# Edge-network pass: the inner layer with its features on the partitions, subtraction and dots on TensorE, floor on ScalarE

## The chip, the core and the metric

The kernel runs on one NeuronCore of a Trainium2 chip. The core has five engines that run side by side: TensorE (matrix products, written to PSUM), VectorE, ScalarE, GpSimd and SyncE; they signal each other by semaphores. The metric is the device time of one execution in microseconds, start to end. TensorE's clock has two levels here, 1.2 and 2.4 GHz; the profile gives the granted clock as a share of the higher one, so that 0.50 is 1.2 GHz.

## What is computed

Four graph layers over 6250 nodes of 128 features and 106,250 edges, sorted by target. The third is the one that matters here:

```python
def _L2_gnn_ref(x, src, dst, W1, b1, W2, b2, W4, b4):
    theta = x[dst] - x[src]
    w = sigmoid(relu(theta @ W1 + b1) @ W2 + b2)        # W2 is 128 x 1
    agg = segment_sum(w * theta, dst)
    indeg = segment_sum(ones, dst)
    return agg + indeg * (x @ W4 + b4)
```

Since theta @ W1 + b1 is (x @ W1 + b1)[dst] - (x @ W1)[src], the layer before it leaves two tables in DRAM: `rows_yh`, with y = x @ W1 and h = x side by side for each node, and `parts_yb`, with x @ W1 + b1 cut into three bf16 parts (high, middle, low) whose sum is the fp32 value.

## The kernel before

`edge_pass` with `edge_net` set is the pass in question. The edges are cut into 832 tiles of 128; 4 tiles are a group (GROUP), 16 a turn (RING, one ring of buffers), so there are 52 turns and 208 groups. In what follows n is a group's number. All targets of a group lie in a window of 64 nodes. The program is unrolled; its order on each engine is that of the code: `over` calls each engine's work for a tile (`tile`, on TensorE `net_tile`) and puts a share of the block's work (`Layer2.on_pe`, `on_dve` and so on, the last product and normalisation of 128 finished nodes) between tiles, at about one block in 4 groups (a step).

What is done for a group, by engine:

- GpSimd (L557): for each tile a gather of 128 rows of `rows_yh` into `ring[:, k]`, edges on the partitions. It may overwrite slot k when by_target of the group that used it is done (`tiles_done`), so it runs up to four groups ahead.
- ScalarE: loads the window's rows of `parts_yb` into `ywin` (L578) and the targets into `relb` (L570); copies by_target out of PSUM (`held_sums`, L585); takes the sigmoid of the dots into `weight` (L597).
- VectorE: `one_hots` makes for 8 tiles `onehot_t` (64 targets on the partitions by edges, L631) and `onehot` (edges by targets, L633). `dots` takes zt - y of the source (L640), the floor at zero times W2, which is spread over all partitions (L643), and the sum over the 128 features (L648). `onehot_w` is onehot times weight (L658). `add_sums` adds the group's sums to `acc` (L687, L689).
- TensorE: `hidden_net` of the next group (L719) spreads the three parts of `ywin` to the edges: per tile three bf16 products into zt[edge, feature] (64 rows contracted, 128 columns); then `turn_sums` of the group before (L729, L730), and `by_target` of this group (L750), four fp32 products that sum weight times h over the edges.

An fp32 product appears in the trace as two weight loads and two products (passes), a bf16 product as one of each.

So within one group's time TensorE runs z of n+1, the turns of n-1 and by_target of n. VectorE runs onehot_w of n, the dots of n+1 and the add of n-1; by_target of n waits for onehot_w of n (semaphore `weighted`), that for the sigmoid (`weight_done`), that for the dots (`dot_done`), those for z (`z_done`). `zt` has two halves, for even and odd groups.

Before the pass, `Layer1.late_dve` makes the y that goes into `rows_yh` (`next_y`), and `expert_tables` loads W2 once.

Of the kernel before, what the change touches and what calls it, by code (L numbers as in the profile page):

```python
# [7 lines left out]
D = 128  # L8
# [4 lines left out]
P = 128  # L13
# [137 lines left out]
def gnn_kernel(nc, t, out):  # L151
    ctx = ExitStack()
    with ctx:
# [284 lines left out]
        def edge_pass(table, width, work, edge_net=None, prologue=None):  # L438
# [11 lines left out]
            with ExitStack() as tmp:  # L450
# [9 lines left out]
                if edge_net:  # L460
                    (w2, b2) = edge_net
                    onehot_t = tmp.enter_context(sbuf("onehot_t", [WIN, 2, HALF * P], B16))
                    relb = tmp.enter_context(sbuf("relb", [WIN, 2, HALF * P]))
                    ywin = tmp.enter_context(sbuf("ywin", [WIN, GROUPS, PARTS * D], B16))
                    hidden = tmp.enter_context(sbuf("hidden", [P, GROUP, D]))
                    dot = tmp.enter_context(sbuf("dot", [P, 2, GROUP]))
# [5 lines left out]
                    names += ["rel_loaded0", "rel_loaded1", "z_done", "net_own", "dot_done", "weight_done",  # L472
                              "weighted", "copied", "turned"] + [f"ywin_loaded{g}" for g in range(GROUPS)]

                def programs(block, sems, loop):
# [87 lines left out]
                    def _(act):  # L563
# [23 lines left out]
                        def tile(i, k):  # L587
                            g, q = divmod(k, GROUP)
                            if edge_net and q == 0:
# [15 lines left out]
                        over(act, tile, flush=(lambda: copy_sums(LAST_GROUP)) if edge_net else None)  # L605
# [14 lines left out]
                    def _(dve):  # L620
# [14 lines left out]
                        def dots(i, g):  # L635

                            n = i * (2 * GROUPS) + 2 * g
                            k = g * GROUP
                            dve.wait_ge(sem["z_done"], i * GROUPS + (g + 1))
                            nc.vector.tensor_tensor(hidden[:, :, :], zt[:, g % 2, :, :], ring[:, k:k + GROUP, 0:D],  # L640
                                                    ALU.subtract).then_inc(sem["net_own"], 1)
                            dve.wait_ge(sem["net_own"], n + 1)
# [4 lines left out]
                            dve.wait_ge(sem["net_own"], n + 2)  # L647
# [3 lines left out]
                        def tile(i, k, ahead=True):  # L651
# [14 lines left out]
                            if edge_net and (ahead or g < GROUPS - 1):  # L666

                                dots(i + (g + 1) // GROUPS, (g + 1) % GROUPS)
# [26 lines left out]
                        if edge_net:  # L695
                            if loop == "edges":
                                nc.vector.memset(ring[:, :, YH:YH + 1], 1.0)
                                dots(0, 0)
                            over(dve, tile, lambda i, k: tile(i, k, ahead=False), lambda: add_sums(LAST_GROUP))
# [4 lines left out]
                    def _(pe):  # L704
# [4 lines left out]
                        def hidden_net(i, k):  # L709
# [23 lines left out]
                        def net_tile(i, k, ahead=True):  # L733

                            g, q = divmod(k, GROUP)
                            if k + GROUP < RING:
                                hidden_net(i, k + GROUP)
# [37 lines left out]
                        if loop == "edges":  # L775
                            pe.sem_inc(tiles_done, RING)
                            if edge_net:
                                for k in range(GROUP):
                                    hidden_net(0, k)
# [226 lines left out]
        class Layer1(Work):  # L1006
# [315 lines left out]
            def late_dve(self, dve, m, i, b):  # L1322
# [30 lines left out]
                m.done("next_y", nc.vector.tensor_copy(s["yh"][:, 0:D], p["misc"][:, 0:D]))  # L1353
# [1270 lines left out]
        w4, b4, w2, b2 = (net.enter_context(sbuf(n, s)) for n, s in (("w4", [P, D]), ("b4", [P, D]), ("w2", [P, D]),  # L2624
                                                                     ("b2", [P, 1])))
        with ExitStack() as lay:
            def weight(name, shape):
# [7 lines left out]
                                    (w2[:, :], bcast_vec(t["L2_gnn_W2"].rearrange("p o -> (p o)"))),  # L2635
# [44 lines left out]
```

## Time and profile before

| | us |
|---|---|
| median of 3 runs | 7054.21 |
| lowest and highest | 7053.46, 7054.47 |
| span of the profiled execution | 8283.1 |

The page knows no other time of the profiled execution than its span from the first to the last instruction. It is 1228.9 us longer than the median of the runs without a profile, so a duration taken from the trace is that of the longer execution. The page gives for every engine busy time, for 40 slices of the span the granted clock of TensorE, and the costliest groups of instructions with the idle time just before them and what ended it. PE is TensorE, PEld its weight loads, DVE VectorE, ACT ScalarE, POOL GpSimd; SPq, ACTq and POOLq are their DMA queues. Idle time that ends with a semaphore is put down to the instruction that released it; semaphores are used again in later phases, so a name such as "DMA acc<-in_edge_type", a load of the setup phase, can stand here for a release that the profile couldn't place.

### The profile page before, as it was taken

How to read it: one execution, taken by the hardware profiler on the slowest of the kernel's cores; microseconds unless marked ns; L12 is line 12 of the kernel's file. 1: busy time of each engine (PE TensorE's matmuls, PEld its weight loads, DVE VectorE, ACT ScalarE, POOL GpSimd, SP SyncE). 2: the span in 40 equal slices, each digit the busy share in tenths (PEclk: the TensorE clock that was granted, in tenths of full speed). 3: DMA queues.
4: the chain of work that ended last, by engine and by line, in shares of the span. 5: the costliest groups of instructions: out<-in, count | busy, mean ns of one | idle time of the engine just before them, and what ended most of it. 6: DMA issues, size and time to landing. Idle time of an engine off the chain costs nothing. (4 is left out here: it accounts for less than half of the span.)

```text
span 8283.1 us, 149959 instructions
## 1 busy us (share of the span) xinstructions
PE 6772.3 (82%) x51098; PEld 4970.7 (60%) x51098; DVE 3911.7 (47%) x11484; ACT 2104.7 (25%) x6166; POOL 3351.8 (40%) x3404
## 2 busy tenths in 40 slices
PE   4999768888886888888688888867767766989899
PEld 2555457676775677677567776755555554545455
DVE  7777534444443444444344554446666662112111
ACT  3555312222221222222133333322222220000000
POOL 0000055555554555555455555536666661000000
PEclk6999879999997999999799999975555557999999
DMA  5444355554444544445444444434444445656565
GB/s 152 139 119 126 115 160 145 143 143 140 140 129 148 143 142 140 138 143 147 133 135 138 141 138 136 139 89 124 128 124 124 126 124 187 196 170 198 175 202 161
DMA packets 714971, 1188.63 MB, mean 144 GB/s; under 512 B 258882, under 2 KB 512998, under 8 KB 712163
## 3 DMA queue, kind: packets, MB, share of 16 engines
q0 software_dynamic: 200640, 601.97, 26.1%
q1 hardware_dynamic: 466786, 447.42, 18.0%
q10 hardware_dynamic: 46784, 129.65, 4.4%
q8 instruction: 411, 6.73, 0.3%
q14 instruction: 350, 2.86, 0.1%
HBM read 993.57 MB, written 185.20 MB: 142 GB/s over the span
## 5 line engine op out<-in xcount | busy, mean ns | idle before, releaser
L557 POOL DMA_INDIRECT ring<-parts,src_idx x2496 | 2452.0, 982 | 1950.7 <-PE sums L707 687.1
L1209 PEld LDWEIGHTS hid<-agg,big 128*128 128x128 f32 x9408 | 1155.6, 196 | 140.2 <-issue 105.9
L1209 PE MATMUL hid<-agg,big 128*128 128x128 f32 x9408 | 1190.6, 280 | 58.8 <-issue 43.5
L2360 PE MATMUL agg_ps<-sheet,big 128*128 128x448 f16 x6174 | 1196.4, 354 | 33.6 <-DMA sheet<-adj 33.6
L1170 PE MATMUL y<-big,strong 128*128 128x256 f32 x4704 | 1126.2, 387 | 40.6 <-issue 21.3
L557 POOL DMA_INDIRECT ring<-rows_yh,src_idx x832 | 838.0, 1007 | 565.4 <-issue 220.3
L677 DVE TENSOR_TENSOR acc<-acc,sums 128x128 f32 x624 | 180.3, 289 | 1678.6 <-DMA acc<-in_edge_type 1171.4
L2360 PEld LDWEIGHTS agg_ps<-sheet,big 128*128 128x128 bf16 x6174 | 605.9, 99 | 582.5 <-DMA sheet<-adj 35.8
L1170 PEld LDWEIGHTS y<-big,strong 128*128 128x128 f32 x4704 | 862.7, 191 | 150.9 <-issue 51.4
L1093 ACT ACTIVATE strong<-hid,s_b 128x128 f32<-128x128 f32 x2352 | 665.3, 368 | 892.6 <-PE hid L1209 615.2
L707 PE MATMUL sums<-onehot,ring 128*128 128x64 bf16 x14976 | 614.5, 196 | 284.1 <-issue 211.6
L707 PEld LDWEIGHTS sums<-onehot,ring 128*128 128x128 bf16 x14976 | 563.2, 100 | 433.6 <-issue 390.5
L1195 PE MATMUL hid<-big,agg 128*128 128x512 f32 x1176 | 747.8, 768 | 64.7 <-DVE agg L1108 53.5
L750 PE MATMUL by_target<-ring,onehot_w 128*64 128x129 f32 x1664 | 408.7, 427 | 131.3 <-DVE onehot_w L658 103.5
L750 PEld LDWEIGHTS by_target<-ring,onehot_w 128*64 128x64 f32 x1664 | 328.5, 223 | 176.9 <-issue 176.3
L1098 DVE SCALAR_TENSOR_TENSOR row<-y,gate,row 128x256 f32<-128x256 f32 x588 | 282.8, 481 | 319.0 <-DMA adj<-big 230.0
L1945 PE MATMUL counts_ps<-hot_col,hot 128*128 128x392 bf16 (+3 forms) x1960 | 348.3, 299 | 102.1 <-DVE hot_col L1804 97.9
L1195 PEld LDWEIGHTS hid<-big,agg 128*128 128x128 f32 x1176 | 254.0, 239 | 272.6 <-issue 212.1
L1073 ACT ACTIVATE weak<-weak 128x512 f32<-128x512 f32 x294 | 185.0, 629 | 866.9 <-DVE weak L1117 778.5
L1776 POOL MEMSET acc<- 128x10976 f32 x1 | 9.2, 9244 | 933.8 <-PE deg_ps L1945 933.8
L2472 DVE SCALAR_TENSOR_TENSOR agg<-agg_ps,counts_hold,acc 128x448 f32<-128x448 f32 x42 | 28.7, 684 | 724.7 <-PE agg_ps L2360 724.7
L2416 POOL MEMSET acc<- 128x448 f32 (+1 forms) x28 | 13.4, 479 | 874.1 <-DVE agg L2472 874.1
(377 smaller groups left out, 8497.9 us busy)
## 6 DMA issues: line engine op xcount, KB each, us to landing
sheet<-adj SPq DMA_DIRECT2D x294, 784.0 KB, 4.2
ring<-parts,src_idx POOLq DMA_INDIRECT x2496
adj<-big ACTq DMA_DIRECT2D x7, 5488.0 KB
adj<-acc ACTq DMA_DIRECT2D x7, 5488.0 KB
hp<-parts SPq DMA_DIRECT2D x147, 192.0 KB
relb<-rel_rows ACTq DMA_DIRECT2D x106, 256.0 KB
parts<-cut SPq DMA_DIRECT2D x99, 192.0 KB, 1.8
h<-rows SPq DMA_DIRECT2D x147, 128.0 KB
```

The source lines that it names most:

```text
L557: nc.gpsimd.indirect_dma_start(ring[:, k, 0:YH] if edge_net else ring[:, k, :], None, table, bass.IndirectOffsetOnAxis(ap=src_idx[:, i * R ...
L677: nc.vector.tensor_tensor(acc[:, 0:n_sums, bass.ds(w, WIN)], acc[:, 0:n_sums, bass.ds(w, WIN)], sums[:, g % 2, 0:n_sums * WIN].rearrange(" ...
L707: return nc.tensor.matmul(ap, lhs, rhs, start=first, stop=last, skip_group_check=True)
L750: last = nc.tensor.matmul(by_target[:, g % 2, 0:D + 1], onehot_w[:, g % 2, j, :], ring[:, g * GROUP + j, D:YH + 1], start=(j == 0), stop=( ...
L1073: m.done(f"relu_w{q}", nc.scalar.activation(both, both, ACT.Relu))
L1093: ins = nc.scalar.activation(s["strong"][:, e % 2, j, :], p["hid"][:, bank_at, j * P:(j + 1) * P], ACT.Relu, bias=self.w["s1_b"][:, e, j:j ...
L1098: m.done(name, nc.vector.scalar_tensor_tensor(out=out, in0=expert, scalar=self.b[0]["gate"][:, e:e + 1], in1=so_far, op0=ALU.mult, op1=ALU ...
L1170: ins = nc.tensor.matmul(y, s["strong"][:, e % 2, k, :], w["s2"][:, k, e, :], start=(k == 0), stop=(k == 3))
L1195: ins = nc.tensor.matmul(hid, s["agg"][:, k, :], w["weak"][:, k, 2 * q:2 * q + 2, :].rearrange("p e f -> p (e f)"), start=(k == 0), stop=( ...
L1209: ins = nc.tensor.matmul(p["hid"][:, bank_at, j * P:(j + 1) * P], w["s1"][:, k, e, j * P:(j + 1) * P], s["agg"][:, k, :], start=(k == 0), ...
L1945: return nc.tensor.matmul(ap, lhs, rhs, start=first, stop=last, skip_group_check=True)
L2360: last = nc.tensor.matmul(ps[:, g % 2, 0:HALF_COLS], now[:, b, c, :], sheet[:, k, s * HALF_COLS:(s + 1) * HALF_COLS], start=(b == 0 and c ...
```

## The change

The inner layer of the network is turned round: features on the partitions, edges along the row.

- `hidden_net`: for a group, three products of `ywin` (as weights) with `onehot_t` over 512 edges give zt[feature, edge]; then for each tile a fp32 product of the gathered y (as weights) with the identity adds to it. `next_y` now stores -y, so this subtracts. z of group n+1 waits in addition for `weight_done` of n-1, since the dots of n-1 stand in the same half of zt. Only the tile products wait for the gathers.
- ScalarE gets `relu_hidden`: the floor of zt, 128 by 512, into `hidden` (two halves now), behind `z_done`.
- TensorE gets `dots`: four fp32 products, `hidden` of a tile as weights with W2 as a single column, into the first four columns of zt; they follow the first tile product of the next group.
- VectorE loses its three steps. The sigmoid reads the dots from PSUM. W2 is loaded as a column of 128 by 1.

```diff
@@ ScalarE @@
-                        def tile(i, k):
+                        def tile(i, k, ahead=True):
...
-                                nc.scalar.activation(weight[:, g % 2, :], dot[:, g % 2, :], ACT.Sigmoid,
+                                nc.scalar.activation(weight[:, g % 2, :], zt[:, g % 2, 0, 0:GROUP], ACT.Sigmoid,
                                                      bias=b2).then_inc(sem["weight_done"], 1)
+                            if edge_net and q == GROUP - 1 and (ahead or g < GROUPS - 1):
+                                relu_hidden(i * GROUPS + g + 1)
+
+                        def relu_hidden(n):
+                            act.wait_ge(sem["z_done"], n + 1)
+                            nc.scalar.activation(hidden[:, n % 2, :], zt[:, n % 2, :, :].rearrange("p q j -> p (q j)"),
+                                                 ACT.Relu).then_inc(sem["hidden_done"], 1)
@@ VectorE @@
-                        def dots(i, g):
...
-                            nc.vector.tensor_tensor(hidden[:, :, :], zt[:, g % 2, :, :], ring[:, k:k + GROUP, 0:D],
-                                                    ALU.subtract).then_inc(sem["net_own"], 1)
...
-                            nc.vector.scalar_tensor_tensor(
-                                out=hidden[:, :, :], in0=hidden[:, :, :], scalar=0.0,
-                                in1=w2.unsqueeze(1).to_broadcast([P, GROUP, D]), op0=ALU.max,
-                                op1=ALU.mult).then_inc(sem["net_own"], 1)
...
-                            nc.vector.tensor_reduce(dot[:, g % 2, :], hidden[:, :, :], AX.X,
-                                                    ALU.add).then_inc(sem["dot_done"], 1)
@@ TensorE, hidden_net @@
-                            pe.wait_ge(gathered[k], i * 16 + 16)
                             if q == 0:
                                 pe.wait_ge(sem[f"ywin_loaded{g}"], i * 16 + 16)
-                            for c in range(PARTS):
-                                last = nc.tensor.matmul(zt[:, g % 2, q, :], onehot_t[:, g // 2, (k % HALF) * P:(k % HALF + 1) * P],
-                                                        ywin[:, g, c * D:(c + 1) * D], start=(c == 0), stop=(c == PARTS - 1))
+                                if not first:
+                                    pe.wait_ge(sem["weight_done"], i * GROUPS + g - 1)
+                                for c in range(PARTS):
+                                    nc.tensor.matmul(zt[:, g % 2, :, :].rearrange("p q j -> p (q j)"), ywin[:, g, c * D:(c + 1) * D],
+                                                     onehot_t[:, g // 2, (k % HALF) * P:(k % HALF + GROUP) * P],
+                                                     start=(c == 0), stop=False, skip_group_check=True)
+                            pe.wait_ge(gathered[k], i * 16 + 16)
+                            last = nc.tensor.matmul(zt[:, g % 2, q, :], ring[:, k, 0:D], ident[:, :], start=False, stop=True,
+                                                    skip_group_check=True)
...
+                        def dots(n):
+                            pe.wait_ge(sem["hidden_done"], n + 1)
+                            for q in range(GROUP):
+                                last = nc.tensor.matmul(zt[:, n % 2, 0, q:q + 1], hidden[:, n % 2, q * P:(q + 1) * P],
+                                                        w2, start=True, stop=True)
+                            last.then_inc(sem["dot_done"], 1)
@@ TensorE, net_tile @@
+                            if q == 0:
+                                dots(n)
...
-                m.done("next_y", nc.vector.tensor_copy(s["yh"][:, 0:D], p["misc"][:, 0:D]))
+                m.done("next_y", nc.vector.tensor_scalar(s["yh"][:, 0:D], p["misc"][:, 0:D], -1.0, None, ALU.mult))
...
-                                    (w2[:, :], bcast_vec(t["L2_gnn_W2"].rearrange("p o -> (p o)"))),
+                                    (w2[:, :], t["L2_gnn_W2"]),
```

The order on the engines. Output<-inputs are the program's names, then the shape of the output; of the semaphores that a row waits for, signal18 is `z_done`, signal19 `net_own` before and `hidden_done` in the change, signal20 `dot_done`, signal21 `weight_done`, signal22 `weighted`, signal23 `copied`, signal2 `added`, signal26 `ywin_loaded1`, signal1 `tiles_done`.

TensorE, one group in the middle of the pass, before:

```order
L719 MATMUL zt<-ywin,onehot_t 128x128 [waits signal26,gathered4]
L719 MATMUL zt<-ywin,onehot_t 128x128 x2
L719 MATMUL zt<-ywin,onehot_t 128x128 [waits gathered5]
L719 MATMUL zt<-ywin,onehot_t 128x128 x2
L719 MATMUL zt<-ywin,onehot_t 128x128 [waits gathered6]
L719 MATMUL zt<-ywin,onehot_t 128x128 x2
L729 MATMUL sums<-ident,held_sums 128x64 [waits signal2,signal23]
L730 MATMUL sums<-ident,held_sums 1x64
L719 MATMUL zt<-ywin,onehot_t 128x128 [waits gathered7]
L719 MATMUL zt<-ywin,onehot_t 128x128 x2
L750 MATMUL by_target<-ring,onehot_w 64x129 [waits signal22,signal23]
L750 MATMUL by_target<-ring,onehot_w 64x129 x3
```

and in the change:

```order
L710 MATMUL zt<-onehot_t,ywin 128x512 [waits signal21,signal26]
L710 MATMUL zt<-onehot_t,ywin 128x512 x2
L714 MATMUL zt<-ident,ring 128x128 [waits gathered4]
L723 MATMUL zt<-w_72,hidden 128x1 [waits signal19]
L723 MATMUL zt<-w_72,hidden 128x1 x3
L714 MATMUL zt<-ident,ring 128x128 [waits gathered5]
L714 MATMUL zt<-ident,ring 128x128 [waits gathered6]
L732 MATMUL sums<-ident,held_sums 128x64 [waits signal2,signal23]
L733 MATMUL sums<-ident,held_sums 1x64
L714 MATMUL zt<-ident,ring 128x128 [waits gathered7]
L755 MATMUL by_target<-ring,onehot_w 64x129 [waits signal22,signal23]
L755 MATMUL by_target<-ring,onehot_w 64x129 x3
```

Twelve products of 128 columns are now three of 512, four more follow with one gather to wait for each, and the four dots stand behind the first of these, with the turns and two tile products between them and by_target.

ScalarE, the group in which a block's square root is taken, before:

```order
L585 COPY held_sums<-by_target 64x129 [waits signal24,signal1]
L597 ACTIVATE weight<-dot,b_73 128x4 [waits signal20]
L898 ACT_TABLE_LOAD
L898 ACTIVATE st<-st 128x1 [waits signal9]
L901 ACTIVATE h_178<-x,st 128x128 [waits signal9]
L503 TENSOR_LOAD step_block
L503 ISA x2
```

and in the change:

```order
L597 ACTIVATE weight<-zt,b_73 128x4 [waits signal20]
L903 ACT_TABLE_LOAD
L903 ACTIVATE st<-st 128x1 [waits signal9]
L906 ACTIVATE h_178<-x,st 128x128 [waits signal9]
L605 ACTIVATE hidden<-zt 128x512 [waits signal18]
L503 TENSOR_LOAD step_block
L503 ISA x2
```

The floor is the last step of each group's turn; in this group of four it stands behind the block's L903 and L906 (L898 and L901 before), and the next group's loads stand behind it.

VectorE, one group, before:

```order
L658 TENSOR_TENSOR onehot_w<-onehot,weight 128x256 [waits signal1,signal21]
L640 TENSOR_TENSOR hidden<-zt,ring 128x512 [waits signal18]
L643 SCALAR_TENSOR_TENSOR hidden<-hidden,w_72 128x512 [waits signal19]
L648 TENSOR_REDUCE dot<-hidden 128x4 [waits signal19]
L684 TENSOR_LOAD win
L684 ISA x2
L687 ISA [waits signal2,signal24]
L687 TENSOR_TENSOR acc<-acc,sums 1x64
L689 ISA
L689 TENSOR_TENSOR acc<-acc,sums 128x64
```

and in the change:

```order
L652 TENSOR_TENSOR onehot_w<-onehot,weight 128x256 [waits signal1,signal21]
L675 TENSOR_LOAD win [waits signal3]
L675 ISA x2
L678 ISA [waits signal2,signal24]
L678 TENSOR_TENSOR acc<-acc,sums 1x64
L680 ISA
L680 TENSOR_TENSOR acc<-acc,sums 128x64
```

The three network steps are gone; onehot_w is followed at once by the add.

## Rows read from the trace of the kernel before

**Rows 1.** The page, part 2: granted TensorE clock in 40 slices, tenths.

```profile
PEclk6999879999997999999799999975555557999999
```

**Rows 2.** One line's own view, for L557 and L719: times, then total us and times of waits.

```profile
  DMA acc<-in_edge_type: 651.3, 337
...
L719 PE MATMUL zt<-ywin,onehot_t x2496: 259/311/311, 5540.9 to 6865.7; 64*128 64x128 bf16 x192
```

**Rows 3.** Busy time by window: PE, PEld, DVE, ACT, POOL, then clock, DMA share, GB/s.

```profile
5700.00:6700.00 1000.00, 707.61 (x3836) 512.62 (x3837) 656.22 (x1656) 241.23 (x610) 634.54 (x630) 0.50 0.45 125
...
5703.34:5714.10 10.76, 10.76 (x58) 7.83 (x58) 4.91 (x12) 1.90 (x8) 7.39 (x8) 0.50 0.44 125
```

**Rows 4.** Groups by line, 5700 to 6700: busy us, mean ns | idle before, by whom.

```profile
L557 POOL DMA_INDIRECT ring<-rows_yh,src_idx x630 | 635.7, 1009 | 365.8 <-issue 167.1 <-DMA acc<-in_edge_type 121.5 <-PE by_target L750 77.2
...
L750 PE MATMUL by_target<-ring,onehot_w 128*64 128x129 f32 x1259 | 309.4, 427 | 102.8 <-DVE onehot_w L658 79.0 <-issue 23.5
...
L643 DVE SCALAR_TENSOR_TENSOR hidden<-hidden,w 128x512 f32<-128x512 f32 x157 | 108.9, 694 | 5.4
...
L648 DVE TENSOR_REDUCE dot<-hidden 128x4 f32<-128x512 f32 x157 | 107.7, 686 | 5.4
...
L640 DVE TENSOR_TENSOR hidden<-zt,ring 128x512 f32<-128x512 f32 x157 | 107.5, 685 | 229.4 <-remote 221.2 <-issue 6.8 <-PE zt L719 1.2
...
L658 DVE TENSOR_TENSOR onehot_w<-onehot,weight 128x256 f32<-128x256 f32 x158 | 67.5, 427 | 34.9 <-issue 21.6 <-ACT weight L597 7.0 <-DMA acc<-in_edge_type 4.0
```

**Rows 5.** Timeline, TensorE, 5707 to 5714: start us, us, instruction.

```profile
5707.10 0.48 PE L1428 MATMUL pb<-ident,agg 128*128 128x128 f32 x1
...
5708.43 1.14 PE L719 MATMUL zt<-ywin,onehot_t 64*128 64x128 bf16 x9
...
5709.36 0.31 PE L729 MATMUL sums<-ident,held_sums 64*128 64x64 f32 x1
...
5709.90 0.50 PE L719 MATMUL zt<-ywin,onehot_t 64*128 64x128 bf16 x3
...
5710.33 1.98 PE L750 MATMUL by_target<-ring,onehot_w 128*64 128x129 f32 x8
...
5712.24 0.80 PE L1434 MATMUL pa<-w,ht 128*128 128x128 f32 x2
...
5712.97 1.14 PE L719 MATMUL zt<-ywin,onehot_t 64*128 64x128 bf16 x9
```

**Rows 6.** Timeline, other engines, 5713 to 5717.

```profile
5713.47 0.94 POOL L557 DMA_INDIRECT ring<-rows_yh,src_idx  x1 [0.30 <-issue]
...
5715.41 0.69 DVE L640 TENSOR_TENSOR hidden<-zt,ring 128x512 f32<-128x512 f32 x1 [5.96 <-remote]
...
5716.94 0.94 POOL L557 DMA_INDIRECT ring<-rows_yh,src_idx  x1 [2.53 <-DMA acc<-in_edge_type]
```

**Rows 7.** Timeline, TensorE, in an expert layer, 2208 to 2222.

```profile
2208.07 1.02 PE L1221 MATMUL misc<-router,ht 128*128 128x9 f32 x4 [0.24 <-ACT ht L1067]
...
2208.95 1.00 PE L1221 MATMUL misc<-router,agg 128*128 128x9 f32 x4
...
2220.16 1.95 PE L1209 MATMUL hid<-agg,big 128*128 128x128 f32 x16
...
2221.95 0.22 PE L707 MATMUL sums<-onehot,ring 128*128 128x64 bf16 x2
```

**Rows 8.** L1073's own view, and ScalarE's timeline at 5721.

```profile
L1073 ACT ACTIVATE weak<-weak x294: 612/630/633, 1117.4 to 5508.9; 128x512 f32<-128x512 f32 x147
...
5721.50 0.20 ACT L898 ACTIVATE st<-st 128x1 f32<-128x1 f32 x1 [2.32 <-DVE st L889]
```

**Rows 9.** Busy time by window, columns as in rows 3.

```profile
64.43:67.87 3.44, 3.39 (x11) 1.39 (x12) 3.44 (x2) 0.00 (x0) 0.00 (x0) 0.50 0.00 0
...
67.87:71.28 3.41, 3.41 (x22) 1.68 (x20) 3.31 (x15) 0.00 (x0) 0.00 (x0) 1.00 0.69 288
...
2208.00:2211.40 3.40, 3.33 (x10) 2.54 (x11) 2.88 (x8) 0.02 (x1) 2.12 (x3) 0.51 0.37 103
```

More of the change, by code:

```diff
@@ L461, in edge_pass @@
                     (w2, b2) = edge_net
+                    assert w2.shape[1] == 1
                     onehot_t = tmp.enter_context(sbuf("onehot_t", [WIN, 2, HALF * P], B16))
@@ L464, in edge_pass @@
                     ywin = tmp.enter_context(sbuf("ywin", [WIN, GROUPS, PARTS * D], B16))
-                    hidden = tmp.enter_context(sbuf("hidden", [P, GROUP, D]))
-                    dot = tmp.enter_context(sbuf("dot", [P, 2, GROUP]))
+                    hidden = tmp.enter_context(sbuf("hidden", [P, 2, GROUP * P]))
                     weight = tmp.enter_context(sbuf("weight", [P, 2, GROUP]))
@@ L471, in edge_pass @@
                     held_sums = tmp.enter_context(sbuf("held_sums", [WIN, 2, D + 1]))
-                    names += ["rel_loaded0", "rel_loaded1", "z_done", "net_own", "dot_done", "weight_done",
+                    names += ["rel_loaded0", "rel_loaded1", "z_done", "hidden_done", "dot_done", "weight_done",
                               "weighted", "copied", "turned"] + [f"ywin_loaded{g}" for g in range(GROUPS)]
@@ L604, in _ @@
                                     load_window(0, k)
-                        over(act, tile, flush=(lambda: copy_sums(LAST_GROUP)) if edge_net else None)
+                                relu_hidden(0)
+                        over(act, tile, lambda i, k: tile(i, k, ahead=False),
+                             flush=(lambda: copy_sums(LAST_GROUP)) if edge_net else None)
                         if edge_net and loop == "edges":
@@ L633, in one_hots, with tile @@
                             nc.vector.tensor_tensor(onehot[:, h, :, :], places, cols, ALU.is_equal).then_inc(onehot_ready, 1)
-                        def dots(i, g):
-                            n = i * (2 * GROUPS) + 2 * g
-                            k = g * GROUP
-                            dve.wait_ge(sem["z_done"], i * GROUPS + (g + 1))
-                            nc.vector.tensor_tensor(hidden[:, :, :], zt[:, g % 2, :, :], ring[:, k:k + GROUP, 0:D],
-                                                    ALU.subtract).then_inc(sem["net_own"], 1)
-                            dve.wait_ge(sem["net_own"], n + 1)
-                            nc.vector.scalar_tensor_tensor(
-                                out=hidden[:, :, :], in0=hidden[:, :, :], scalar=0.0,
-                                in1=w2.unsqueeze(1).to_broadcast([P, GROUP, D]), op0=ALU.max,
-                                op1=ALU.mult).then_inc(sem["net_own"], 1)
-                            dve.wait_ge(sem["net_own"], n + 2)
-                            nc.vector.tensor_reduce(dot[:, g % 2, :], hidden[:, :, :], AX.X,
-                                                    ALU.add).then_inc(sem["dot_done"], 1)
-                        def tile(i, k, ahead=True):
+                        def tile(i, k):
                             g, q = divmod(k, GROUP)
@@ L665, in tile @@
                                 return
-                            if edge_net and (ahead or g < GROUPS - 1):
-                                dots(i + (g + 1) // GROUPS, (g + 1) % GROUPS)
                             if edge_net:
@@ L697, in _ @@
                                 nc.vector.memset(ring[:, :, YH:YH + 1], 1.0)
-                                dots(0, 0)
-                            over(dve, tile, lambda i, k: tile(i, k, ahead=False), lambda: add_sums(LAST_GROUP))
+                            over(dve, tile, flush=lambda: add_sums(LAST_GROUP))
                         else:
@@ L707, in tile_sum, with hidden_net @@
                             return nc.tensor.matmul(ap, lhs, rhs, start=first, stop=last, skip_group_check=True)
-                        def hidden_net(i, k):
+                        def hidden_net(i, k, first=False):
                             g, q = divmod(k, GROUP)
@@ L736, in net_tile @@
                             if k + GROUP < RING:
-                                hidden_net(i, k + GROUP)
+                                hidden_net(i, k + GROUP, first=i * GROUPS + g < 1)
                             elif ahead:
@@ L778, in _ @@
                                 for k in range(GROUP):
-                                    hidden_net(0, k)
+                                    hidden_net(0, k, first=True)
                         if edge_net:
@@ L2623, in gnn_kernel @@
         net = ctx.enter_context(ExitStack())
-        w4, b4, w2, b2 = (net.enter_context(sbuf(n, s)) for n, s in (("w4", [P, D]), ("b4", [P, D]), ("w2", [P, D]),
+        w4, b4, w2, b2 = (net.enter_context(sbuf(n, s)) for n, s in (("w4", [P, D]), ("b4", [P, D]), ("w2", [P, 1]),
                                                                      ("b2", [P, 1])))
```

## The prediction

> **What bounds the kernel now.** I read the page first: TensorE's clock row stands at 7 to 9 nearly everywhere, but at 5 in one block of six slices [rows 1]. That block is the edge-network pass: its products over zt start between 5540.9 and 6865.7 [rows 2], so 208 groups of four tiles take some 1325 us. The change touches nothing else that runs often. In the 1000 us from 5700 TensorE was busy 707.61 us at a clock of 0.50 (1.2 GHz), VectorE 656.22, ScalarE 241.23 and GpSimd 634.54 [rows 3]. The by_target products came 1259 times, 8 to a group, so there were 157 groups: 6.37 us each, of which TensorE worked 4.5, VectorE 4.2, GpSimd 4.0.
>
> Who waits for whom is in the groups by line: by_target stood idle for 102.8 us of these 1000, 79.0 of them for onehot_w, and GpSimd for 365.8 us before its gathers [rows 4]. VectorE's three network steps cost 685 + 694 + 686 ns = 2.07 us a group [rows 4], but the products of the next group and the sums of this one run meanwhile. **So no engine is full**; the pass is a ring of handovers in which TensorE is the longest member, and that in its slow clock.
>
> One wait I can't name. In the turn that I show, TensorE's last product for zt starts at 5709.90 and by_target ends by 5712.31 [rows 5], but L640, which needs zt alone, starts at 5715.41 after 5.96 us of idleness, and the gather that needs by_target's slots at 5716.94 [rows 6]. GpSimd has 337 such waits, 651.3 us, in the whole span [rows 2], so it isn't this pass alone. The profiled execution spans 1228.9 us more than the median of 7054.21; these stalls may be what profiling adds. I carry them both ways below.
>
> **The change, part by part** (a group; durations from start to start at clock 0.50).
>
> *TensorE, before.* z: nine products in 0.93 us and three in 0.43, 1.36. The two turns 0.54. by_target 1.91. The block's work, once in a little over four groups, 1.33 + 0.73, so 0.5 [rows 5]. Sum 4.3.
>
> *z turned round.* Twelve products of 128 columns become three of 512: the same 1536 columns. Nine weight loads go, but they lay beside products. 1.3 us, gain 0 to 0.1.
>
> *The subtraction.* It adds four fp32 products, 128 by 128, two passes each. From below: by_target's eight passes of 129 columns took 1.91, 0.24 a pass, so 0.48 a product. The same shape (L1209) at full clock ran 16 passes in 1.79 us, 0.11 each, doubled 0.22, which says the same. From above: L1434, same shape at 0.50 but standing alone, its weight load not hidden, took 0.73 [rows 5, 7]. Four cost 1.9 to 2.9; I take 1.9, since they follow other products whose time hides the load, as in L1209.
>
> *The dots.* Four fp32 products with one column, so only weights are loaded: eight passes. L1221 (nine columns, clock 0.50) started its next four passes 0.88 us after the first four, 0.22 a pass; with the end of the last counted in, 1.02 or 0.26 [rows 7]. 1.8 to 2.1; I take 1.8, the pace of a row of them.
>
> TensorE after: 1.3 + 1.9 + 1.8 + 0.54 + 1.91 + 0.5 = **8.0 us a group** (7.9 to 9.3), 3.7 more.
>
> *VectorE* loses 2.07 us a group. Nobody is served by that: it had 2.1 us to spare.
>
> *ScalarE* gains a floor over 128 by 512; L1073, a ScalarE step of that shape, took 630 ns in the median [rows 8]. It isn't waited for: between z_done(n) and dots(n) stand by_target(n-1), z and one subtraction, 1.91 + 1.3 + 0.5 us. After the dots come three subtractions and the turns, 2.0 us, before by_target asks for weights that need one short ScalarE step and 0.43 us of onehot_w [rows 4]: hidden, but for the table load that the sigmoid has once a step. In one group of four the floor is queued behind the block's square root (L898, L903 in the change), which waits for VectorE's statistics, 2.32 us in the row [rows 8]; those now come sooner, as VectorE is freer. The order has as many table loads as before, so the floor adds none. z's new wait for weight_done(n-1) is met a by_target earlier.
>
> *Gathers.* z no longer waits for them, only the subtraction does; the wait moves inside the same group, nothing gained. The column load of W2 and the sign in next_y cost the same within a microsecond in all.
>
> *Sum.* TensorE goes from 4.5 busy plus 1.9 idle to 8.0 to 8.2 busy plus whatever idleness is left. If all hidden waits go and the unnamed stall too, a group is 8.2 and the profiled pass grows 208 x (8.2 - 6.37) = 381 us; if the stall stays (about 4 us in four groups, 1.0), 9.2 and 589 us. For runs without a profile I scale the pass by 7054/8283: 1325 becomes 1128 us, 5.42 a group. TensorE alone then sets 8.0: 208 x 8.0 = 1664, **+536 us**, 7590. From that I take off 20 us for short stretches at full clock: **7570**.
>
> **The clock** decides. In the pass now TensorE never left 0.50, not even from 5703.34 to 5714.10, when it was busy for all of 10.76 us [rows 3]. Its products there use half the array: z has 64 of 128 rows, by_target 64 of 128 columns. Elsewhere products with 128 rows but a single column of weights (L1550, the only ones there) raised the clock: 0.50 from 64.43 to 67.87, then 1.00 [rows 9]. So the columns of weights don't seem to matter, and the rows may; then z's 64 rows hold the clock down. The new subtractions have all 128 rows, the new dots keep the array idle while weights are loaded: when such products (L1221, from 2208.07) led a row of dense ones, the clock stood at 0.51 from 2208 to 2211.4 with TensorE busy for 3.33 of 3.40 us [rows 7, 9]. The group thus has 1.3 us of z with half the rows, 1.8 of dots with nearly nothing, and 3.8 of full rows. I think that is at the border, mostly below.
> The Trainium skill ("TensorE: Matmul & The Clock Gate", Part 1) says that the throttled state is the default and that sustained activity releases it. Taken plainly, a TensorE that is busy without gaps, as after the change, would go to 2.4 GHz, which is rival 2; the row of 10.76 us speaks against taking it plainly.
>
> **Rivals.**
> 1. *The clock alternates.* A third of the groups pass at full clock at some 5.4 us, the others at 8.0: 7.15 in the mean, 208 x (7.15 - 5.42) = +360: 7415. For it: full-row products stand together from the second subtraction to by_target. Against: the dots in every group.
> 2. *The clock rises and stays (the other side).* TensorE needs 4.0 us a group; then GpSimd's gathers bound, 4 x (1.009 + 0.30) = 5.2 [rows 4, 6], with handovers 5.2 to 5.6, where 5.42 stands now: -45 to +40, **7060**. It decides as soon as a group's idle time and dots together don't pull the clock down. Against it: at full clock TensorE would idle for 1.2 of 5.2 us and stand in the dots' weight loads for another 0.9.
> 3. *Weight loads exposed.* Subtractions at 0.73 as L1434, since each waits for its own gather, dots at 0.26: 9.3 a group at most, 9.0 more likely: +745, 7800.
> 4. *VectorE's relief counts.* The 79 us that by_target waited for onehot_w come back, and more; at most 0.5 us a group [rows 4], 104 us, which doesn't change the sign while the clock is 0.50. It is inside the range.
>
> **How the numbers follow.** Forecast, mostly 0.50: 0.50 (7500 to 7680). Rival 1: 0.22 (7330 to 7500). Rival 2: 0.13. Rival 3: 0.15 (7680 to 7850). The range 7380 to 7740 holds the forecast, most of rival 1 and a third of rival 3. Faster or slower by over 0.2% (14 us) is about what a measurement of this kernel tells from no change; rival 2 splits into 0.04 faster, 0.04 same and 0.05 slower, all else is slower: 0.04, 0.04, 0.92.
>
> **What would show it.** In the profile after: the pass some 1700 to 1900 us long, TensorE over 85% busy in it, clock 0.50 to 0.55; subtraction passes 0.24 us apart, dot passes 0.22; ScalarE's floor about 630 ns; VectorE near 2.2 us a group; by_target's wait for onehot_w near nothing. GpSimd idle over 3 us a group. A clock of 0.7 in the pass means rival 1, one of 0.95 and gathers back to back rival 2, spacing over 0.3 us at 0.50 rival 3. I am wrong if the rows of the array are not what counts for the clock.

## Result: 7.4% slower, at the predicted time

| | us |
|---|---|
| kernel before, median of 4 runs | 7054.34 (7053.46 to 7065.89) |
| changed kernel, median of 4 runs | 7579.26 (7559.20 to 7611.94) |
| ratio | 1.0741, 95% interval 1.0722 to 1.0760 |
| predicted | 7570 (7380 to 7740), slower 0.92 |
| span of the profiled execution, changed | 7564.4 |

The page of the changed kernel, part 2 (40 slices of 189 us: busy tenths of TensorE and VectorE, then the clock). The pass is in slices 24 to 32 (counted from 0), where TensorE is full and the clock stands at 5 to 6; in [rows 1] it stood at 5 in the pass:

```profile
PE   3999959999979999979999989999999979989899
...
DVE  7777726665646666646666652222222222222111
...
PEclk6999979999989999989999995556555569999999
```

One line's own view for the tile zt (first and last start of a line's instructions): the pass runs from 4554.0 to 6151.0, 1597 us or 7.68 a group.

```profile
L714 PE MATMUL zt<-ident,ring x1664: 274/421/582, 4555.4 to 6147.2; 128*128 128x128 f32 x185
...
L723 PE MATMUL zt<-w,hidden x1664: 168/352/374, 4559.6 to 6151.0; 128*128 128x1 f32 x185
...
L710 PE MATMUL zt<-onehot_t,ywin x624: 373/630/632, 4554.0 to 6141.2; 64*128 64x512 bf16 x156
L605 ACT ACTIVATE hidden<-zt x208: 572/597/598, 4557.8 to 6147.7; 128x512 f32<-128x512 f32 x104
```

Busy time by window (PE, PEld, DVE, ACT, POOL, clock, DMA share, GB/s), the row that answers to [rows 3]: TensorE was busy for 986 of 1000 us. VectorE has 287 us, 2.2 a group.

```profile
4700.00:5700.00 1000.00, 986.49 (x4137) 706.69 (x4138) 287.14 (x991) 273.03 (x643) 513.73 (x527) 0.58 0.36 105
```

The groups by line in the same 1000 us, 132 groups (before: [rows 4]). The dots wait 9.8 us for the floor and by_target 3.4 for onehot_w, so the new chain over three engines is hidden. VectorE now waits 621.7 us for the weights.

```profile
L557 POOL DMA_INDIRECT ring<-rows_yh,src_idx x527 | 514.6, 976 | 486.6 <-PE by_target L755 356.0 <-issue 130.5
L714 PE MATMUL zt<-ident,ring 128*128 128x128 f32 x1056 | 331.6, 436 | 0.0
L755 PE MATMUL by_target<-ring,onehot_w 128*64 128x129 f32 x1052 | 237.7, 399 | 3.4 <-DVE onehot_w L652 3.4
...
L723 PE MATMUL zt<-w,hidden 128*128 128x1 f32 x1056 | 198.4, 309 | 9.8 <-ACT hidden L605 9.8
...
L605 ACT ACTIVATE hidden<-zt 128x512 f32<-128x512 f32 x132 | 78.1, 591 | 157.1 <-PE zt L714 156.2
L652 DVE TENSOR_TENSOR onehot_w<-onehot,weight 128x256 f32<-128x256 f32 x132 | 56.2, 426 | 621.7 <-ACT weight L597 621.7
```

And the timeline of TensorE over two groups (start us, us, instruction), to be set beside [rows 5]:

```profile
5003.31 1.32 PE L710 MATMUL zt<-onehot_t,ywin 64*128 64x512 bf16 x3
5004.57 0.49 PE L714 MATMUL zt<-ident,ring 128*128 128x128 f32 x2
5004.96 1.05 PE L723 MATMUL zt<-w,hidden 128*128 128x1 f32 x8
5005.88 0.69 PE L714 MATMUL zt<-ident,ring 128*128 128x128 f32 x4
5006.50 0.27 PE L732 MATMUL sums<-ident,held_sums 64*128 64x64 f32 x1
...
5008.20 1.95 PE L755 MATMUL by_target<-ring,onehot_w 128*64 128x129 f32 x8 [0.81 <-DVE onehot_w L652]
5010.08 1.46 PE L710 MATMUL zt<-onehot_t,ywin 64*128 64x512 bf16 x3
5011.47 0.79 PE L714 MATMUL zt<-ident,ring 128*128 128x128 f32 x2
5012.06 1.71 PE L723 MATMUL zt<-w,hidden 128*128 128x1 f32 x8
5013.62 1.20 PE L714 MATMUL zt<-ident,ring 128*128 128x128 f32 x4
5014.75 0.37 PE L732 MATMUL sums<-ident,held_sums 64*128 64x64 f32 x1
5015.05 0.37 PE L733 MATMUL sums<-ident,held_sums 64*1 64x64 f32 x2
5015.35 0.79 PE L714 MATMUL zt<-ident,ring 128*128 128x128 f32 x2
5016.07 0.48 PE L755 MATMUL by_target<-ring,onehot_w 128*64 128x129 f32 x1
```

The reader sees both levels of the clock. From 5008.20 to 5016.07 TensorE works at 1.2 GHz (granted clock 0.50) and a group without a block's work takes 7.87 us: by_target 1.88, z 1.39, subtractions 0.59 + 1.13 + 0.72 = 2.44, dots 1.56, turns 0.60. In the group before it two subtractions took 0.62 us (5005.88 to 5006.50) at 2.4 GHz. A little later the same trace shows how the clock falls again:

```profile
5029.16 0.95 PE L723 MATMUL zt<-w,hidden 128*128 128x1 f32 x8
5029.97 0.69 PE L714 MATMUL zt<-ident,ring 128*128 128x128 f32 x4
5030.59 0.28 PE L732 MATMUL sums<-ident,held_sums 64*128 64x64 f32 x1
...
5035.64 1.87 PE L723 MATMUL zt<-w,hidden 128*128 128x1 f32 x8 [1.96 <-ACT hidden L605]
```

```profile
5028.30:5035.10 6.80, 5.38 (x35) 3.60 (x33) 3.48 (x11) 2.24 (x5) 5.24 (x6) 1.00 0.33 97
5035.10:5044.00 8.90, 8.36 (x33) 6.13 (x33) 2.12 (x9) 3.15 (x7) 3.39 (x5) 0.50 0.45 127
```

At full clock TensorE reached the dots before ScalarE had the floor ready, waited 1.96 us, and the clock fell to 0.50 in that wait. By the trace's record of the granted clock it fell 18 times in the pass. Just before 9 of these falls TensorE had waited, 6 times for the floor and 3 times for onehot_w; before the other 9 it hadn't waited (0.08 us at most).

### The profile page after: what moved, and what is told of

The parts are those of the page before. It is cut to its first block and busy times, and to the rows that moved or that the text cites. A ratio compares the mean times of both kernels' runs of the same rounds, so it can differ in the third digit from the quotient of the medians.

```text
span 7564.4 us, 152407 instructions
## 1 busy us (share of the span) xinstructions
PE 7059.2 (93%) x52554; PEld 5254.0 (69%) x52554; DVE 3500.6 (46%) x10860; ACT 2225.0 (29%) x6374; POOL 3318.3 (44%) x3404
## 3 DMA queue, kind: packets, MB, share of 16 engines
q0 software_dynamic: 200640, 601.97, 27.9%
## 5 line engine op out<-in xcount | busy, mean ns | idle before, releaser
L557 POOL DMA_INDIRECT ring<-parts,src_idx x2496 | 2445.4, 980 | 976.1 <-issue 712.9
L557 POOL DMA_INDIRECT ring<-rows_yh,src_idx x832 | 811.1, 975 | 850.7 <-PE by_target L755 563.0
L1214 PEld LDWEIGHTS hid<-agg,big 128*128 128x128 f32 x9408 | 1113.2, 192 | 51.3 <-issue 37.2
L1214 PE MATMUL hid<-agg,big 128*128 128x128 f32 x9408 | 1133.7, 276 | 0.0
L697 PEld LDWEIGHTS sums<-onehot,ring 128*128 128x128 bf16 x14976 | 534.0, 99 | 210.1 <-issue 129.2
L697 PE MATMUL sums<-onehot,ring 128*128 128x64 bf16 x14976 | 560.0, 195 | 99.7 <-DMA ring<-parts,src_idx 95.9
L1200 PE MATMUL hid<-big,agg 128*128 128x512 f32 x1176 | 587.2, 623 | 0.0
L652 DVE TENSOR_TENSOR onehot_w<-onehot,weight 128x256 f32<-128x256 f32 x208 | 88.5, 426 | 1003.1 <-ACT weight L597 1003.1
L714 PE MATMUL zt<-ident,ring 128*128 128x128 f32 x1664 | 530.1, 441 | 0.4 <-DMA ring<-rows_yh,src_idx 0.2
L714 PEld LDWEIGHTS zt<-ident,ring 128*128 128x128 f32 x1664 | 373.6, 293 | 196.2 <-issue 190.6
L755 PE MATMUL by_target<-ring,onehot_w 128*64 128x129 f32 x1664 | 382.0, 404 | 4.6 <-DVE onehot_w L652 4.6
```

Source lines behind the costliest of these rows:

```text
L557: nc.gpsimd.indirect_dma_start(ring[:, k, 0:YH] if edge_net else ring[:, k, :], None, table, bass.IndirectOffsetOnAxis(ap=src_idx[:, i * R ...
L697: return nc.tensor.matmul(ap, lhs, rhs, start=first, stop=last, skip_group_check=True)
L714: last = nc.tensor.matmul(zt[:, g % 2, q, :], ring[:, k, 0:D], ident[:, :], start=False, stop=True, skip_group_check=True)
L755: last = nc.tensor.matmul(by_target[:, g % 2, 0:D + 1], onehot_w[:, g % 2, j, :], ring[:, g * GROUP + j, D:YH + 1], start=(j == 0), stop=( ...
L1200: ins = nc.tensor.matmul(hid, s["agg"][:, k, :], w["weak"][:, k, 2 * q:2 * q + 2, :].rearrange("p e f -> p (e f)"), start=(k == 0), stop=( ...
L1214: ins = nc.tensor.matmul(p["hid"][:, bank_at, j * P:(j + 1) * P], w["s1"][:, k, e, j * P:(j + 1) * P], s["agg"][:, k, :], start=(k == 0), ...
```

## Experiments

**e1: the kernel before, profiled again.** No edit.

> The kernel before, profiled once more. The trace that the prediction rests on spans 8283.1 us against a median of 7054.34, that of the changed kernel 7564.4 against 7579.26. Theory A: the unnamed stalls (L640 5.96 us idle behind a finished z) belonged to that one execution; this one spans 7050 to 7070, the pass takes some 1085 us (5.2 a group) and GpSimd's waits under 'DMA acc<-in_edge_type' are near none. Rival: profiling this kernel costs that much each time; the span is 8200 to 8300 again.

Measured 7063.56 us, span 7061.8. Theory A holds: the trace that the prediction was made from had stalls of its own. The view of L557 here and, from the timeline at 5000, GpSimd's gathers:

```profile
L557 POOL DMA_INDIRECT ring<-rows_yh,src_idx x832: 942/946/1482, 4562.7 to 5639.2; - x167
...
  issue: 945.1, 3089
...
  PE by_target L750: 16.8, 55
```

```profile
5004.82 0.94 POOL L557 DMA_INDIRECT ring<-rows_yh,src_idx  x1 [0.30 <-issue]
5006.06 0.94 POOL L557 DMA_INDIRECT ring<-rows_yh,src_idx  x1 [0.30 <-issue]
```

GpSimd gives out gather after gather 0.30 us apart, and has waited 16.8 us for by_target in the whole pass, where [rows 2] told of 337 waits under the name of the setup load (651.3 us); that name isn't in this answer. zt's products start from 4566.7 to 5646.4: 1080 us, 5.19 a group (4 gathers of 995 ns and 0.30). **What bounded the kernel before was GpSimd**. TensorE worked 515 of 600 us in 4800 to 5400; it waited 35.0 us for gathers and 27.9 for onehot_w:

```profile
L557 POOL DMA_INDIRECT ring<-rows_yh,src_idx x463 | 460.5, 995 | 141.1 <-issue 131.9 <-PE by_target L750 9.1
L750 PE MATMUL by_target<-ring,onehot_w 128*64 128x129 f32 x922 | 227.7, 428 | 27.9 <-DVE onehot_w L658 27.9
L719 PE MATMUL zt<-ywin,onehot_t 64*128 64x128 bf16 x1389 | 199.3, 305 | 36.3 <-DMA ring<-rows_yh,src_idx 35.0 <-SPq L148 0.3
```

What stalled the first traced execution isn't known; none of the timed runs of this kernel was near 8283 us. The stalls also hid how busy VectorE was: 481 of 600 us here, against 656 of 1000 in [rows 3].

**e2 and e3: z over 128 rows.** In the changed kernel and in the kernel before:

```diff
-onehot_t = ... sbuf("onehot_t", [WIN, 2, HALF * P], B16)
-ywin = ... sbuf("ywin", [WIN, GROUPS, PARTS * D], B16)
+onehot_t = ... sbuf("onehot_t", [P, 2, HALF * P], B16)
+ywin = ... sbuf("ywin", [P, GROUPS, PARTS * D], B16)
...
+                            if edge_net:
+                                nc.vector.memset(ywin[WIN:P, :, :], 0.0)
+                                nc.vector.memset(onehot_t[WIN:P, :, :], 0.0)
```

(The load of `ywin` and the step that writes `onehot_t` go to the first 64 rows, as before.)

> The changed kernel, but z contracts 128 rows instead of 64: the lower halves of ywin and onehot_t are zeros, set once. Same products, same durations, same result. Theory (rows of the array in use hold the clock down): the clock of the pass goes from 0.57 to over 0.9, a group from 7.66 us to 5.3 to 5.7, the run to 7070 to 7160. Rival (TensorE's idle time or the dots' weight loads hold it down, not the rows): clock 0.55 to 0.6, 7580 within 20.

> The kernel before with the same 128 rows in z. by_target keeps its 64 columns of weights. Theory (rows count, columns don't): the clock rises from 0.50 for part of the pass, 0.6 or more; time 7000 to 7055, since GpSimd's gathers (5.0 us a group) leave little to gain. Rival 1 (rows times columns count): by_target still fills half the array, clock 0.50 throughout, 7054 within 10. Rival 2 (neither counts): the same 0.50.

Measured: e2 7255.46 us, ratio to the kernel before 1.0277 (1.0260 to 1.0294), so 324 us less than the change; e3 7064.37, ratio 1.0003 (0.9993 to 1.0013). Windows of e2 and then e3, each from its own trace:

```profile
4800.00:5400.00 600.00, 550.00 (x2969) 431.31 (x3017) 206.36 (x720) 198.59 (x470) 374.85 (x387) 0.75 0.46 129
```

```profile
4800.00:5000.00 200.00, 154.81 (x946) 111.75 (x946) 163.01 (x408) 59.59 (x151) 152.90 (x155) 0.66 0.58 154
```

The clock rose from 0.57 to 0.75 and from 0.50 to 0.66 though only zeros were added. That the rows of z count is shown; that they alone hold it at 0.57 is not, for e2 missed both its clock (over 0.9) and its time (7070 to 7160). In e3 by_target kept its 64 columns and the clock rose nevertheless, so by_target's half array alone doesn't keep it at 0.50; since z gained rows and area at once, e3 doesn't tell rows from rows times columns. And TensorE, busy 155 instead of 172 of 200 us, bought e3 nothing: it wasn't the bound.

What stood before each fall can be read from e2's trace: the clock fell 43 times in the pass, and each time TensorE had just waited, 37 times for the floor. At full clock the chain over ScalarE and VectorE is no longer hidden, as in the rows at 5035.64 above. That these waits bring the clock down is read from the order in time; no run takes them away.

Not all of e2's 324 us are the clock's. Here is z, the first subtraction and the dots of e2 at clock 0.50 (4827.63 to 4829.31):

```profile
4827.63 1.46 PE L713 MATMUL zt<-onehot_t,ywin 128*128 128x512 bf16 x3
4828.89 0.63 PE L717 MATMUL zt<-ident,ring 128*128 128x128 f32 x2
4829.31 1.71 PE L726 MATMUL zt<-w,hidden 128*128 128x1 f32 x8
```

From z to the dots it takes 1.68 us, in the change 1.98 (5010.08 to 5012.06), at the same clock. In the change the first weight load of the subtraction starts at 5011.47, when z's last product, started at 5010.91, is nearly through; in e2 it starts at 4828.46 together with that product. So the weights of a 128-row product were loaded in the open behind 64-row products, 0.3 us a group, at most some 60 us in the pass.

**e4: no subtraction.** The four tile products left out, `z_done` on the third product of z.

> The changed kernel without the four subtraction products of each group; the gathers are still waited for. Leaves out the subtraction of the source's y. Theory (1.9 us a group at clock 0.50, on the path): the clock stays at 0.50, a group goes from 7.66 to some 5.9 us, minus 1.8 x 208 = 370: 7210, 7170 to 7260. Rival (weight loads exposed, 0.73 a product): 7000 to 7060. Rival (off the path): 7500 or more.

Measured 7382.84, ratio 1.0456 (1.0435 to 1.0477): 196 us less than the change, half of what was expected. On the path it is, but two things took from it. The clock was 0.50 in the whole pass, where the change had 0.57; the subtraction's products are all that went. And waits came that the subtractions had hidden:

```profile
L752 PE MATMUL by_target<-ring,onehot_w 128*64 128x129 f32 x704 | 171.2, 424 | 38.0 <-DVE onehot_w L652 38.0
L720 PE MATMUL zt<-w,hidden 128*128 128x1 f32 x711 | 164.4, 352 | 14.0 <-ACT hidden L605 12.8
```

52 us of waits in 88 groups, 0.6 a group, where the change had 0.1; a group took 6.8 us.

**e5: one dot of four.** `for q in range(1)` in `dots`.

> The changed kernel with one of the four dot products of each group. Leaves out three quarters of the dots, so the weights of three tiles in four are not the reference's. Theory (the dots cost 0.22 us a pass and, standing in weight loads, hold the clock down): 6 passes less are 1.3 us at the same clock, 7305; the clock rises above 0.57 as well, so 7130 to 7290, clock 0.65 to 0.9. Rival (dots cost their time and nothing else): clock within 0.03 of 0.57 and 7305 within 20.

Measured 7357.92, ratio 1.0416 (1.0395 to 1.0437), 221 us less than the change; 90 groups in 600 us, 6.7 each, and the clock of that window 0.57 as in the change. On the clock the rival was right; the time is 53 us longer than it said, since the six passes cost 0.195 us each at 0.50 and some 0.10 at full clock, and not 0.22: at 0.57 some 1.1 us a group, 230 us in the pass. Taking three dots of four away doesn't raise the clock here. But it isn't a clean test of what the dots do to the clock: the clock fell 27 times in this pass, 25 times just behind a wait for the floor (6 of 18 in the change), and with less work in a group more of that chain is in the open.

**e6: wide dots.** W2's column is streamed 128 times over:

```diff
-last = nc.tensor.matmul(zt[:, n % 2, 0, q:q + 1], hidden[:, n % 2, q * P:(q + 1) * P],
-                        w2, start=True, stop=True)
+last = nc.tensor.matmul(zt[:, n % 2, q, :], hidden[:, n % 2, q * P:(q + 1) * P],
+                        w2.to_broadcast([P, P]), start=True, stop=True)
...
-zt[:, g % 2, 0, 0:GROUP], ACT.Sigmoid
+zt[:, g % 2, :, 0], ACT.Sigmoid
```

> The changed kernel with W2's column repeated 128 times as the moving side of each dot product (a step of zero, no copy): 128 columns of result instead of one, of which the sigmoid reads the first. A pass of the dots is bound by its weight load (0.22 us at clock 0.50), under which 128 columns, two for one, fit. Theory (what the array does, not what TensorE waits for, sets the clock): the clock goes from 0.57 to over 0.9, a group from 7.66 us to 5.2 to 5.6, the run to 7055 to 7150, though it computes more. Rival: clock as now, the time the same or up to 100 us longer for the added columns, 7560 to 7680.

Measured 7157.40, ratio 1.0136 (1.0113 to 1.0160): 422 us less than the change, by streaming 128 times as many columns in the dots. The clock of the pass (window 4800 to 5400) and the dots in the timeline:

```profile
4800.00:5400.00 600.00, 541.39 (x3325) 392.41 (x3325) 228.46 (x799) 218.44 (x518) 412.99 (x425) 0.92 0.52 141
```

```profile
5007.60 1.06 PE L723 MATMUL zt<-w,hidden 128*128 128x128 f32 x8
5008.49 0.61 PE L714 MATMUL zt<-ident,ring 128*128 128x128 f32 x4
5009.03 0.27 PE L732 MATMUL sums<-ident,held_sums 64*128 64x64 f32 x1
```

At full clock the eight passes of 128 columns take 0.89 us, where those of one column took 0.81 in the change (5029.16 to 5029.97); the two subtractions behind them take 0.54 instead of 0.62. Together it is 1.43 us in both, and in the median over the pass the two also agree at 0.50 (2.70 us): the added columns cost no time. z still has its 64 rows here, and TensorE's row of products takes as long as in the change at either level, so these 422 us are the clock's. The 24 falls that are left in this pass all follow a wait of TensorE, 19 of them for the floor.

**e7: both.**

> Both: z over 128 rows (lower halves zero) and the wide dots. Theory: full clock nearly throughout, over 0.95, and GpSimd's gathers bound again at 5.2 us a group as in the kernel before: 7055 to 7090. Rival (ScalarE's queue or the handovers between ScalarE, TensorE and VectorE bound at full clock): full clock and 5.5 us or more, 7120 to 7200.

Measured 7079.42, ratio 1.0023 (1.0013 to 1.0032). Clock 0.96, 5.3 us a group, and GpSimd is nearly back at its pace (28.6 us of waits for by_target in 600):

```profile
4800.00:5400.00 600.00, 522.24 (x3502) 413.23 (x3557) 246.18 (x858) 232.29 (x551) 443.40 (x455) 0.96 0.55 150
```

```profile
L557 POOL DMA_INDIRECT ring<-rows_yh,src_idx x455 | 443.8, 975 | 156.9 <-issue 128.3 <-PE by_target L758 28.6
...
L726 PE MATMUL zt<-w,hidden 128*128 128x128 f32 x911 | 129.0, 285 | 44.1 <-ACT hidden L605 44.1
L758 PE MATMUL by_target<-ring,onehot_w 128*64 128x129 f32 x904 | 128.4, 286 | 22.5 <-DVE onehot_w L652 22.4
```

So the two edits, which take no product away, give back 500 of the change's 525 us. Of these 422 are the clock's (e6); the other 78 are the clock and the shorter way from z to the subtraction (e2) together. Near the full clock the change costs 15 us over the kernel before, since TensorE's added work then nearly fits beside GpSimd's gathers.

**e8: fewer waits before the gathers**, in the kernel before.

```diff
-                                pool.wait_ge(tiles_done, i * RING + (k + 1))
-                                pool.nop(nofuse=True)
+                                if k % GROUP == 0:
+                                    pool.wait_ge(tiles_done, i * RING + (k + 1))
+                                    pool.nop(nofuse=True)
```

> The kernel before, in which GpSimd waits for free slots once a group, not before each of its four gathers (tiles_done rises by four, so the other three waits never wait), with the empty instruction behind the wait left out as well. In all four edge passes. Theory (GpSimd's issue of gathers, 1.25 to 1.3 us each, bounds the edge-network pass of the kernel before): what is saved per gather shows whole in the pass; if the 0.30 us between gathers is partly wait and empty instruction, 0.05 to 0.15 us a gather, 40 to 120 us in this pass and as much again in the others at most: 6850 to 7020. Rival (0.30 us is the gather instruction's own): 7060 within 8, gathers still 0.30 apart.

Measured 7063.28, ratio 1.0000 (0.9990 to 1.0010). The gathers still stand 0.30 us apart (135.1 us idle under "issue" before 464 gathers, 131.9 before 463 without the edit), so neither the wait nor the empty instruction makes them: the rival was right.

**e9 and e10: dots one tile later**, on top of e7 (`if q == 1: dots(n)`), and that with e8's edit.

> The changed kernel with z over 128 rows and wide dots, and the dots behind the second tile product instead of the first. At full clock TensorE waited 44.1 us in 600 for the floor before the dots (0.39 us a group). Theory: that wait goes, GpSimd bounds alone, 7079 becomes 7060 to 7070. Rival (the weights then come late for by_target): 7079 or more, with by_target's wait for onehot_w up from 22 us in 600.

> Both of the above. If gathers get cheaper, TensorE's 4.3 us at full clock leave more room than the 4.5 us at 0.50 of the kernel before; theory: 0 to 30 us below the kernel before with the same gathers. Rival (ScalarE's and VectorE's handovers bound at 5 us a group): above it.

Measured 7132.41, ratio 1.0098 (1.0077 to 1.0119), and 7134.30, 1.0100 (1.0083 to 1.0117). The wait for the floor stayed (38.9 us in 600) and by_target's wait for onehot_w didn't rise (21.1), so neither reason given holds, and e10's gain didn't come either; the clock fell from 0.96 to 0.92. In e9's pass it fell 33 times, 25 of them behind a wait for the floor, against 15 and 11 in e7, though both have 46 waits for the floor of over 1.0 us. So not every such wait brings a fall, and why the later order has more of them isn't settled. No version that does the whole work beats the kernel before.

**e11: three gathers a group**, in the kernel before.

```diff
+                                if edge_net and k % GROUP == GROUP - 1 and i > 0:
+                                    continue
```

(TensorE doesn't wait for the fourth gather either, from the second turn on.)

> The kernel before with three gathers a group instead of four in the edge-network pass, from the second turn on; the fourth slot keeps the rows of the first turn. Leaves out a quarter of the source rows. Theory (GpSimd's four gathers of 1.29 us each bound the pass at 5.2 us a group): the bound moves to TensorE's 4.5 us at clock 0.50 with its waits, 4.6 to 4.9 us a group, minus 60 to 120 us: 6945 to 7005. Rival (TensorE or the handovers bound it already): 7055 or more. With it stands or falls the step of the prediction that took TensorE for the longest member.

Measured 7030.71, ratio 0.9961 (0.9947 to 0.9975): 28 us less, between the two and half of the theory's least. Gathers bounded, for leaving one out gained; but they bounded only 0.14 us a group ahead of what comes next. That is a ring of TensorE's 4.4 us at 0.50 and its handovers, which now show:

```profile
L559 POOL DMA_INDIRECT ring<-rows_yh,src_idx x355 | 350.8, 988 | 248.7 <-PE by_target L752 157.2 <-issue 91.5
L752 PE MATMUL by_target<-ring,onehot_w 128*64 128x129 f32 x950 | 234.1, 427 | 40.6 <-DVE onehot_w L660 40.0 <-issue 0.6
```

## Why the prediction was right, and where it wasn't

The sign, the size and the mechanism came as forecast: 208 groups on a TensorE that is full, mostly at 1.2 GHz. That the time lies within 10 us of the forecast is luck, as the terms show. Point by point:

- *VectorE's 2.07 us are worth nothing*: it fits all traces. VectorE went from 4.2 to 2.2 us a group and waits, and e7, with VectorE as free and the clock near full, isn't faster than the kernel before either. But it had 1.0 us a group to spare (5.19 less 4.2, e1) and not 2.1.
- *The chain floor, dots, sigmoid, onehot_w is hidden*: right, 9.8 and 3.4 us of waits in 1000. It is hidden only by slow products: at full clock (e7) it cost 0.6 us a group, 44.1 + 22.5 us in 113 groups, and the waits then go together with falls of the clock (e2, e6).
- *TensorE 8.0 us a group at 0.50*: 8.4 (7.87 and 0.5 of the block's work). z 1.39 for 1.3, turns 0.60 for 0.54. **The subtraction was mis-sized**: 2.44 us for 1.9, inside its ends of 1.9 and 2.9. I took the pace of by_target and of a long row of one shape; here the products stand in ones and twos between z and the turns, which have 64 rows, and 0.3 us of the miss are the weight load in the open behind z (e2). The dots were mis-sized the other way, 1.56 for 1.8.
- *Clock 0.50, 20 us off for short stretches*: 0.57 over the pass. A seventh of the time at the full clock brings 8.4 to 7.68, 0.7 us a group or some 150 us. It is between the forecast and rival 1.
- *The end of the pass.* The group's terms were some 80 us too short and the clock some 130 too slow: 1644 us forecast, 1597 measured, 47 too long.
- *The starting point.* I scaled 1325 us of a stalled trace to 1128; the true pass is 1080 (e1), 48 less. The two errors cancel: the pass grew by 517 us, and 516 were forecast.
- *"TensorE is the longest member"* of the ring before: wrong. GpSimd is, by 0.14 us (e1, e11). The unnamed stall hid it, for it made GpSimd look idle for 365.8 of 1000 us. But the number stood in rival 2: gathers of 5.2 us a group against TensorE's 4.5. It did no harm to the sum, since TensorE in the change is far above both.
- *The signs.* The pass was to take 1700 to 1900 us and took 1597; the clock was to be 0.50 to 0.55 and was 0.57; subtraction passes were to be 0.24 us apart and are 0.28 to 0.36, dot passes 0.22 and are 0.20. TensorE's share, the floor (597 ns), VectorE's time, by_target's wait and GpSimd's idle time (3.7 us a group) came as said.
- *The rows of the array count for the clock*: right as far as it went (e2, e3). But z's 64 rows don't hold it down by themselves: in e6 they are as they were, and the clock is 0.92. That the idle array under the dots' weight loads holds it down fits e6; e5, which removed three quarters of them, doesn't decide it. Two things lower the clock in these traces: the kind of products, since in the change it fell 9 times though TensorE hadn't waited, and waits, since in e2, e6 and e7 each fall follows one. How they add up isn't shown.
- In 1000 us of the change TensorE was busy for 98.6% and the granted clock was 0.58. The Trainium skill ("TensorE: Matmul & The Clock Gate", Part 1) says that sustained activity releases the throttle. Taken as busy time, that fails in this row; that the falls in e2, e6 and e7 follow waits agrees with it.
- *Rival 2* was right in what it said of the full clock: 7060 forecast, 7079 measured in e7.

## What to carry to other kernels

Price a step that is moved to TensorE at the clock that the stage grants, and look at the clock row beside the busy row: here the change costs 525 us near the low level and, with two edits that only fill the array, 15 near the full one. An engine that isn't the bound (VectorE, 4.2 of 5.2 us busy) has nothing to give. Before believing which engine is the bound, take the trace twice when its span is far from the median, and count the time between an engine's instructions as its own where no wait explains it (GpSimd's 0.30 us). Where a TensorE stage is full and stays in the low clock, try to fill what is idle in the array: zeros in the unused rows, a repeated column under a weight load. It pays only where TensorE is the bound (e3 gained nothing).

## What the hardware did that I had not expected

- More work ran faster: repeating one column 128 times under the weight loads took the pass from clock 0.57 to 0.92 and the run from 7579 to 7157 us (e6).
- Zeros in 64 unused rows raised the clock by 0.16 to 0.18 (e2, e3), and behind such a z the next weight load started 0.3 us earlier at clock 0.50 (e2).
- The first traced execution of the kernel before spanned 8283.1 us, 17% over its runs, and no later trace of any kernel here was more than 2 us from its run.
